# Gated cross-attention block with a quantised FFN: the order of two late groups of softmax denominators

## The reference

```
def xattn(q, k, v):                 # q = layernorm(x), k = v = ctx
    q, k = rope(q), rope(k)
    scores = einsum('bqhd,bkhd->bhqk', q, k) / sqrt(32) + alibi_bias
    attn = softmax(scores, axis=-1)
    return einsum('bhqk,bkhd->bqhd', attn, v)

x = x + tanh(g_xattn) * xattn(layernorm(x), ctx, ctx)
x = x + tanh(g_ffn) * ffn(layernorm(x), w_gate, w_up, w_down)
```

## Time and profile before

| what | us |
|---|---|
| median of 3 runs | 1759.76 (1759.01 to 1761.27) |
| profiled execution, its own time | 1760.35 |
| span of the profile | 1758.6 |
| PE busy | 1604.0 (91%) |
| POOL busy | 838.7 (48%) |
| first and last start of the denominators on PE (L1041) | 79.2 and 913.4 |

### The profile page before, as it was taken

The page is one execution under the profiler, slowest core; times in us unless marked ns, Lnnn a source line. Parts: engine busy times, 40 slices in busy tenths (PEclk is TensorE's granted clock), DMA queues, the critical chain, the costliest instruction groups (busy, mean ns, idle before and its releaser), DMA issues. The chain is left out here.

```text
span 1758.6 us, 37266 instructions
## 1 busy us (share of the span) xinstructions
PE 1604.0 (91%) x14821; PEld 637.0 (36%) x14821; DVE 1450.8 (82%) x2082; ACT 1221.8 (69%) x1941; POOL 838.7 (48%) x504
## 2 busy tenths in 40 slices
PE   3899999999999999999969999999999950899999
PEld 0233333333333333333315444444444420344444
DVE  7899999999999888889857997868989989755451
ACT  3688888888899888988743332328997987754450
POOL 4699899999999999998830010100000000000000
PEclk9999999999999999999989999999999985899999
DMA  6678888888799787778467888849998999986661
GB/s 154 155 147 178 163 172 181 167 170 173 151 178 182 152 171 157 167 151 160 95 168 195 254 253 252 228 153 322 349 344 276 331 347 387 303 270 218 220 216 60
DMA packets 377182, 367.94 MB, mean 209 GB/s; under 512 B 217872, under 2 KB 288912, under 8 KB 369072
## 3 DMA queue, kind: packets, MB, share of 16 engines
q1 hardware_dynamic: 368080, 300.55, 61.5%
q0 software_dynamic: 8928, 65.02, 18.8%
HBM read 154.08 MB, written 95.42 MB: 142 GB/s over the span
## 5 line engine op out<-in xcount | busy, mean ns | idle before, releaser
L1462 DVE TENSOR_REDUCE cm<-quad 128x1 f16<-128x1024 f32 x512 | 600.7, 1216 | 63.2 <-PE quad L1004 62.2
L1243 ACT ACTIVATE P<-quad 128x512 f32<-128x512 f32 x1024 | 556.9, 598 | 112.5 <-PE quad L1017 100.8
L2069 POOL TENSOR_TENSOR Ps<-P,P 128x2048 f32<-128x2048 f32 x93 | 440.3, 4735 | 43.8 <-ACT P L1243 43.8
L1017 PE MATMUL quad<-QA,KA 101*32 101x512 f16 x4096 | 366.0, 385 | 6.8 <-ACT P L1243 5.3
L1004 PE MATMUL quad<-KA,QA 100*32 100x512 f16 x4096 | 334.4, 391 | 35.5 <-DMA QA<-S 18.1
L1068 PE MATMUL quad<-P,cg 128*32 128x512 f32 x2048 | 265.4, 594 | 0.0
L1096 PE MATMUL quad<-x_hl,Wg 128*128 128x512 f16 (+1 forms) x1200 | 249.6, 370 | 5.4 <-DMA x_hl<-xs 4.3
L1096 PE MATMUL quad<-x_hl,Wu 128*128 128x512 f16 x1152 | 248.8, 379 | 0.0
L1157 PE MATMUL quad<-Wd,oh 128*128 128x512 f16 x768 | 228.6, 379 | 0.0
L1017 PEld LDWEIGHTS quad<-QA,KA 101*32 101x32 f16 x4096 | 105.1, 94 | 298.8 <-ACT P L1243 231.3
L1324 ACT ACTIVATE ev<-quad 128x1024 f32<-128x1024 f32 x95 | 96.3, 1014 | 125.5 <-PE quad L1096 119.4
(11 more groups left out here) (169 smaller groups left out, 1937.0 us busy)
## 6 DMA issues: line engine op xcount, KB each, us to landing
Ps<-P POOLq DMA_DIRECT2D x62, 1024.0 KB, 8.1
gate_scratch<-ev SPq DMA_DIRECT2D x48, 512.0 KB, 3.7
gt<-gate_scratch SPq DMA_DIRECT2D x48, 512.0 KB, 5.4
up_scratch<-ev SPq DMA_DIRECT2D x48, 512.0 KB, 4.5
ud<-up_scratch SPq DMA_DIRECT2D x96, 256.0 KB, 3.6
x_words<-up_scratch SPq DMA_DIRECT2D x45, 512.0 KB, 11.4
gated_scratch<-gq SPq DMA_DIRECT2D x48, 256.0 KB, 4.2
gd<-gated_scratch SPq DMA_DIRECT2D x96, 128.0 KB, 4.2
```

The lines of the kernel that those rows point to most:

```text
L1017: mm = e.matmul(K.score[h % 2][j:j + 32, :], K.KA[p % 2][0:101, kt, h, j:j + 32], K.QA[p % 2][0:101, 4 * qc:4 * qc + 4, h, :], start=True, ...
L1243: e.activation(K.Pb[pb][:, h, :], K.score[h % 2], ACT.Exp, scale=SCALE / (QPOW * KPOW)).then_inc(K.a_exp, 1)
L1462: e.tensor_reduce(cm[:, col:col + 1], K.quad[UNIT["max", hm, u] % 2][:, :], AX.X, ALU.max).then_inc(K.v_max, 1)
L2069: e.tensor_tensor(K.Ps[n][:, :, :], K.Pb[(st.g - 1) % NP][:, :, :], K.Pb[st.g % NP][:, :, :], ALU.add).then_inc(K.g_sum, 1)
```

## The change

Of the three groups of denominators of a half, the last two change places. Tiles 3 to 5 (`n` = 2, `Ps[2]`) come in step 1 of the next half, and tiles 6 and 7 (`n` = 1, `Ps[1]`) in step 2. The count in `pe_den`, the flag that ends the accumulation in PSUM, and the wait of ACT for the last group follow. The wait inside each group stays as it is: n = 1 waits for POOL's sum (`g_sum`), n = 2 for the accumulating DMA (`d_acc[1]`).

```
         elif s in (1, 2) and 1 <= hf < NHALF:
-            self.dens = (hf - 1, s)
+            self.dens = (hf - 1, 3 - s)

 def den_no(hf, n):
-    return 3 * hf + n + 1
+    return 3 * hf + (n if hf == NHALF - 1 else (0, 2, 1)[n]) + 1

     def denominators(hf, n):
...
-            mm = e.matmul(..., start=n == 0, stop=n == (3 if hf == NHALF - 1 else 2))
+            mm = e.matmul(..., start=n == 0, stop=n == (3 if hf == NHALF - 1 else 1))

         if st.den_out is not None:
-            e.wait_ge(K.pe_den, den_no(hf, 3 if hf == NHALF - 1 else 2))
+            e.wait_ge(K.pe_den, den_no(hf, 3 if hf == NHALF - 1 else 1))
```

More of the change, by code:

```diff
@@ L1040, in denominators @@
                 e.wait_ge(K.v_sum, 5)
-            mm = e.matmul(K.den[32 * h:32 * h + 32, :], K.ones[:, :], K.Ps[n % 2 if hf == NHALF - 1 else n][:, h, :], start=n == 0, stop=n == (3 if hf == NHALF - 1 else 2))
+            mm = e.matmul(K.den[32 * h:32 * h + 32, :], K.ones[:, :], K.Ps[n % 2 if hf == NHALF - 1 else n][:, h, :], start=n == 0, stop=n == (3 if hf == NHALF - 1 else 1))
         mm.then_inc(K.pe_den, 1)
```

## The result

| | before | after |
|---|---|---|
| median, us | 1759.31 (14 runs) | 1765.83 (14 runs, 1761.01 to 1770.38) |
| ratio, 95% interval | | 1.0034 [1.0024, 1.0045] |
| profiled execution, own time | 1760.35 | 1762.93 |
| span of the profile | 1758.6 | 1761.1 |

The change makes the kernel slower by 4 to 8 us. I had forecast 1760.6 and no change that can be measured; the median lies above my range. The single times spread over 9 us, where those of the kernel before spread over 6.

The account below looks back on a forecast made before the run. PE, busy for 91% of the span, was taken as the bound, with POOL setting the pace from 508.8 to 809.5 us. Terms +1.3 -0.1 +0.1 -0.3 +0.1 -0.3 sum to +0.8: 1760.6 us, range 1756.0 to 1764.5.

Parts of the forecast that it names:

- What goes: PE's 14 waits for POOL's sum, all in a step 1, go entirely: 6.7 us of idle time at most.
- the late stretch: 508.8 to 809.5 us, halves 17 to 28: POOL sets the pace; of 4.1 us of waits only -0.3 us is left.
- What comes: In step 1 PE waits for the accumulating DMA issued in step 6: late in 15 of 31 places, 8.8 us in all.
- A delay of PE moves POOL only at the next point where POOL is idle for want of an exponential.: Rule for adding terms: between such points POOL's issues stay, and a later wait for POOL or its DMA absorbs the delay.
- the terms of halves 1 and 2: Step 1: half 1 makes PE 1.3 us late, half 2 absorbs that delay; +1.3 us for the two, not 1.3 + 1.2.
- Half 10, term 0: PE starts 1.1 us later in step 1, but a 1.17 us wait for a DMA in step 6 absorbs it: 0.
- The other halves: Half 4 -0.1, half 6 +0.1, half 12 -0.3, half 16 +0.1, half 28 -0.3 us; halves 29 to 31 0.
- The upper bound: Nothing is absorbed: 8.8 us of lateness less 6.7 us of waits for POOL, +2.1 us.
- A: Rival, chance 0.12: DMAs of step 6 land later; from +0.4 us each it costs +3.7 us, 1763.5.
- B: Rival, chance 0.06: the DMAs' data are there in time nearly everywhere, -4.6 us, 1755.2.
- C: Rival, 0.82 together with the forecast: POOL is the only limit, old waits return elsewhere, halves 1 and 2 lose nothing; 0, 1759.8.

Follow-up runs that it names:

- the filled kernel: The changed kernel with 16 more matmuls with zeros on PE ahead of the wait in halves 1, 2 and 10: 1763.17 us, 1.0028.
- its version with the loads moved: The kernel before, with SP's loads of two tiles of x (256 KB each) two steps earlier: 1757.74 us, 0.9993.

## Why the prediction was wrong

- **What goes.** Right: the wait for POOL went in all places. Right too that the late stretch gives nothing back for it: halves 16 to 30 alone gave 1.0004 for 4 us of waits removed. That POOL sets the pace there is borne out.
- **What comes.** Right in place and nearly in size: halves 1, 2 and 10 have the large waits, 1.2 to 2.1, 1.6 to 2.6 and 1.3 to 1.7 us in the traces, where I had read 1.3, 1.6 and 1.5 (327.3 less 325.8).
- **"A delay of PE moves POOL only at the next point where POOL is idle for want of an exponential."** This is the step that failed. POOL also waits for DVE's row statistics in half 1, and DVE goes in step with PE (1.8 us later in the first trace, behind a wait of 1.88). I had looked only at where POOL was idle before. Here DVE's result was there only 0.2 us ahead of its use, and a delay of 1.2 to 1.9 us made POOL wait 0.8 to 1.5. So the terms of halves 1 and 2 add up. I had +1.3 for the two; the traces show +2.5 without the lower clock, +2.8 in the first trace and +3.3 on average.
- **Half 10, term 0.** Failed too: the absorption rested on a wait in step 6 that one trace had by chance of a landing. The second has none, nor have the six of the changed kernel, and the measured term is 1.1 to 1.6 us on average, 0.6 to 1.1 in the four traces without a lower clock there.
- **The price of a wait.** This term I had at nothing, without a reason: I had priced each wait at its length. Behind some, TensorE ran at 1.2 GHz for a while, for 1.7 us more. By the table this makes most of the difference between 56 and 58 us from half 0 to half 2.
- **The other halves.** From half 11 to half 27 +0.2 us in the traces, against my -0.2 (-0.3 and +0.1); from half 27 to half 31 -0.6, against -0.3.
- **The upper bound.** +2.1 us was no bound. It let all 6.7 us of waits for POOL count as given back, against my own argument for the late stretch. Halves 1 to 17 alone, read the same way from the same trace, are late by 6.0 us against 2.6 us of waits, which gives +3.4.
- **The rivals.** A had the right side, but its mechanism, later landings throughout, isn't what happened: the DMAs of step 6 took 8.7 us on average in both traces of before and 8.7 to 8.8 in the six of the changed kernel. B (faster) is out by the time, and C by the waits in halves 1 and 2.

Open: in the attention the three traces of the changed kernel without a stretch at the lower clock average 2.8 us above the two of before, and all six 4.0 us, while the two medians of the changed kernel lie 6.5 us above those of the kernel before. So the traces show 4 us of the gap, and not the rest. The three slowest of the 14 (1769.6 to 1770.4 us) had a mean granted clock of 0.972 to 0.974, the three fastest (1761.0 to 1761.4) 0.976 to 0.977. This fits more stretches at 1.2 GHz in the long ones, as in the long execution of the filled kernel. But the kernel before, which has none of them in its traces, also has a lower mean clock in its longer executions (0.9756 on average above 1761.5 us, 0.9772 below 1758). The trace of its version with the loads moved, at 1762.05 us, runs at 1.2 GHz for 24 us between 909 and 1002 us, the passage to the FFN and what follows, where the two traces of before do so for 14. This is a rival for a part of the rest. And no execution of the changed kernel above 1766 us has a trace. So that part is argued and not shown.

## What to carry to other kernels

To move a wait from a compute engine to a DMA, put issue plus landing of each single place beside the time at which the reader is ready, and of more than one trace: here 3 of 31 places made all of the loss that could be measured. Before a delay is called absorbed, list everything that the other engine waits for, also where it isn't waiting now but has less than the delay to spare (here 0.2 us). And a stall ahead of matmuls can cost more than its length.

## What I had not expected of the hardware

TensorE fell to its lower clock inside a stage in which it is 96% busy, behind single waits of 1.33 to 2.65 us, in some executions and not in others at the same place (two groups of 8 matmuls at 1.83 and 1.95 us in place of 1.06 and 1.04). An accumulating DMA of 1 MB took from 6.8 to 12.1 us to land over all traces here; moving two loads of 256 KB out of the way of one took about 1 us off it (from 10.7 to 9.6).
